# A half-width tile moved from the end of a matmul stage to its start, and the reload behind it

## The reference

```python
x = x + (x @ W.T + b + (x @ (2 * mask - 1)) * coeff)          # layer 0, mask per sequence
def lora_add(base, inp, A, B):                                # A, B picked per sequence
    t = einsum('bri,bni->bnr', A, inp)
    return base + einsum('bor,bnr->bno', B, t) * 0.5
gate = lora_add(x @ W_gate.T, x, A_gate, B_gate)              # 1024 -> 2752
up   = lora_add(x @ W_up.T,   x, A_up,   B_up)
act  = silu(gate) * up
x = x + lora_add(act @ W_down.T, act, A_down, B_down)         # 2752 -> 1024
```

## Time and profile before

| | |
|---|---|
| runs | 1579.68 us median of 3 (1578.99 to 1580.78) |
| span of the profiled execution | 1579.3 us; what lies around the span is not shown apart |
| PE busy | 1545.1 us, 98% |
| DVE, ACT, POOL busy | 1220.1 us (77%), 802.3 us (51%), 426.1 us (27%) |
| moved by DMA | 325.66 MB, 206 GB/s over the span |
| stages | layer 0 to 201 us; block 0 gate/up to 675, down to 889; block 1 gate/up to 1362, down to the end |

### The profile page before, as it was taken

The page is one execution under the profiler, slowest core; times in us unless marked ns, Lnnn a source line. Parts: engine busy times, 40 slices in busy tenths (PEclk is TensorE's granted clock), DMA queues, the critical chain, the costliest instruction groups (busy, mean ns, idle before and its releaser), DMA issues.

```text
span 1579.3 us, 23432 instructions
## 1 busy us (share of the span) xinstructions
PE 1545.1 (98%) x7550; PEld 1304.1 (83%) x7550; DVE 1220.1 (77%) x2136; ACT 802.3 (51%) x1478; POOL 426.1 (27%) x821
## 2 busy tenths in 40 slices
PE   6999998999999999999999989999999999999999
PEld 6999986888888888878888868888888888778887
DVE  8999887676666677688888887767766667798886
ACT  8999855444444444443334464444444444443332
POOL 0000142333333333253410024332323233443100
PEclk9999999999999999999999999999999999999999
DMA  9999854444444444699593725444444445996653
GB/s 372 374 361 376 322 172 127 147 137 154 144 139 155 156 157 153 230 334 312 168 375 111 241 78 168 157 139 134 148 152 148 131 157 179 316 374 220 216 196 116
DMA packets 141961, 325.66 MB, mean 206 GB/s; under 512 B 22416, under 2 KB 50320, under 8 KB 141840
## 3 DMA queue, kind: packets, MB, share of 16 engines
q0 software_dynamic: 61216, 176.21, 33.4%
q1 hardware_dynamic: 76016, 139.57, 26.0%
q10 hardware_dynamic: 4608, 8.39, 1.4%
HBM read 233.51 MB, written 90.18 MB: 205 GB/s over the span
## 4 chain that ended last, share of the span: by engine, by line
PE 87%; DVE 7%; issue 2%; ACT 2%; DMA 1%; SPq 1%; ACTq 0%; POOL 0%; DVEq 0%
PE ps L1509 59%; PE ps L1505 26%; PE ps L1645 2%; DVE m_raw L1135 1%; DVE m_lo L1132 1%; DVE op_b L1132 1%; DMA acc<-x_scratch 1%; DVE acc L1135 1%; DMA m_raw<-in_mask 1%; DVE lo L1132 1%; ACT hi L791 0%; DVE fx L1132 0%; SPq L512 0%; DVE raw L1132 0%; DVE act_t L1306 0%
## 5 line engine op out<-in xcount | busy, mean ns | idle before, releaser
L1509 PE MATMUL ps<-op_b,hi 128*128 128x512 f32 x1616 | 503.4, 393 | 9.3 <-DVE u L1135 5.6
L1132 DVE TENSOR_TENSOR lo<-raw,hi 128x512 fp32r<-128x512 f32 (+2 forms) x640 | 333.4, 530 | 128.7 <-ACT hi L791 126.7
L791 ACT ACTIVATE hi<-raw 128x512 fp32r<-128x512 f32 (+1 forms) x592 | 304.9, 519 | 220.9 <-PE ps L1509 182.9
L1509 PEld LDWEIGHTS ps<-op_b,hi 128*128 128x128 f32 x1616 | 306.0, 190 | 74.1 <-DVE u L1135 6.4
L1509 PE MATMUL ps<-op_b,lo 128*128 128x512 f32 x808 | 318.0, 394 | 0.0
L1509 PE MATMUL ps<-op_d,hi 128*128 128x512 f32 x800 | 248.5, 392 | 4.4 <-DVE acc L1135 4.1
L1505 PE MATMUL ps<-op_b,hi 128*128 128x512 f32 x816 | 252.0, 390 | 0.0
L638 POOL DMA_DIRECT2D operand_scratch<-ot x140 | 75.3, 541 | 552.4 <-DVE ot L1132 536.1
L1135 DVE TENSOR_TENSOR acc<-acc,ps 128x512 f32<-128x512 f32 x248 | 169.9, 685 | 51.0 <-PE ps L1509 43.3
L1509 PEld LDWEIGHTS ps<-op_d,hi 128*128 128x128 f32 x800 | 147.8, 188 | 39.8 <-DVE acc L1135 9.8
L1505 PEld LDWEIGHTS ps<-op_b,hi 128*128 128x128 f32 x816 | 153.4, 188 | 30.7
(11 more groups left out here) (130 smaller groups left out, 2315.9 us busy)
## 6 DMA issues: line engine op xcount, KB each, us to landing
operand_scratch<-ot POOLq DMA_DIRECT2D x140, 512.0 KB, 3.9
op_d<-operand_scratch POOLq DMA_DIRECT2D x140, 512.0 KB, 10.9
raw<-in_wgu SPq DMA_DIRECT2D x168, 256.0 KB, 3.8
m_raw<-in_mask SPq DMA_DIRECT2D x64, 512.0 KB, 5.9
raw<-in_wd SPq DMA_DIRECT2D x160, 128.0 KB, 4.7
w_in<-in_w SPq DMA_DIRECT2D x32, 512.0 KB, 6.7
x_scratch<-x_out POOLq DMA_DIRECT2D x32, 256.0 KB, 4.8
acc<-x_scratch POOLq DMA_DIRECT2D x16, 512.0 KB, 7.5
```

Of the source, the lines that this page charges most:

```text
L791: return nc.scalar.activation(o, i, ACT.Copy)
L1132: return nc.vector.tensor_tensor(o, a, b, ALU.subtract)
L1509: return mm(dst, weight, v, start=False, stop=stop, skip_group_check=True)
```

## The change

The half tile is computed second, right after tile 0, plainly (two "q" steps for each half of the columns, each with the weights of one half of the inner dimension) and in one bank for each half. The adapter's up rows are brought into the form that tiles 2 and later use before tile 1, not between tiles 1 and 2. The operands of down segment 0 have other places in SBUF, so that most of their loads may start earlier in tile 20; the load of acc row 1 is issued after them. Down's banks take turns the other way round. The table b_gu is permuted on the host so that the half tile's adapter rows come second.

```diff
-FUSED = ["q1", "q2", "q3", "q4"]
+HALF_TILE = ["q1", "q2"]
-OPERAND_AT = ["t4", "b11", "t1", "t2", "b22", "t3", "b21"]
+SEG_AT = [{"b11": 8, "t1": 9, "t2": 6, "b22": 7, "t3": 4, "b21": 5, "t4": 10},
+          {"b11": 0, "t1": 1, "t2": 2, "b22": 3, "t3": 11, "b21": 12, "t4": 13}]
 # first_tile_steps: what ACT and DVE do behind a step of PE
-            ("ta", 1, 1): forms("t2", 0, 1, 2, 3) + a_part(1, 6),
-            ("r", 0): [("result", 0)],
-            ("h", 1, 5): [("make4", 2), ("make4", 3)] + forms("t4", 2, 3),
-            ("ta", 1, 7): [("t sum", 1)] + forms("t3", 0),
-            ("g", 1, "p1"): [("t own", 1), ("t high", 1), ("t low", 1)] + forms("t3", 1),
-            ("g", 1, "p5"): [("lora_b", 1)] + forms("t3", 2, 3) + [("make4", 0), ("make4", 1)],
-            ("g", 1, "p6"): forms("t4", 0, 1),
+            ("ta", 1, 1): [("lora_b", PAIRS)] + forms("t2", 0, 1) + a_part(1, 6),
+            ("r", 0): [("result", 0)] + forms("t2", 2, 3),
+            ("h", 1, 5): [("make4", 2), ("make4", 3)],
+            ("ta", 1, 7): [("t sum", 1), ("t own", 1), ("t high", 1), ("t low", 1)],
+            ("q", 0, 0): forms("t3", 0, 1, 2, 3),
+            ("q", 0, 1): [("half result", 0)],
+            ("q", 1, 0): [("make4", 0), ("make4", 1)] + forms("t4", 2, 3),
             ("r", 1): [("result", 1)],
-            ("g", 1, "p3"): [("second result",), ("t neg",)]}
+            ("q", 1, 1): [("half result", 1), ("lora_b", 1)] + forms("t4", 0, 1) + [("half keep", 0), ("half keep", 1)],
+            ("g", 1, "p1"): [("second result",)]}
 # pe_order
-        order += [("g", s, 1, u) for u in PRODUCTS[:3]] + [("r", s, 1)]
-        order += [("g", s, 1, u) for u in PRODUCTS[3:6]] + [("td", s, 0), ("g", s, 1, "p4")]
+        order += [("q", s, 0, 0), ("q", s, 0, 1), ("q", s, 1, 0), ("r", s, 1), ("q", s, 1, 1)]
+        order += [("g", s, 1, u) for u in PRODUCTS[:6]] + [("td", s, 0), ("g", s, 1, "p4")]
-        order += [("g", s, PAIRS, u) for u in FUSED[:2]] + [("td", s, PAIRS - 1)]
-        order += [("g", s, PAIRS, u) for u in FUSED[2:]]
 # POOL, tile 20
-                            pool.wait_ge(pe_done, done["g", s, PAIRS - 1, "p5"])
-                            load_operand(s, 0, "p1")
-                            load_operand(s, 0, "p5")
+                            for u in PRODUCTS[:6]:
+                                pool.wait_ge(pe_done, done["g", s, PAIRS - 1, {"p1": "p5", "p7": "p3", "p2": "p3", "p3": "p6"}.get(u, u)])
+                                load_operand(s, 0, u)
-                pool.wait_ge(ot_l, ot_index[s, KP - 1, "t4"] + 1)
+                pool.wait_ge(pe_done, done["g", s, PAIRS - 1, "p7"])
+                load_operand(s, 0, "p4")
                 load_acc(s, 1)
-                pool.wait_ge(pe_done, done["g", s, PAIRS - 1, "p7"])
-                load_operand(s, 0, "p6")
-                load_operand(s, 0, "p3")
                 ... wait for all stores of ot, load_acc(s, 0) ...
-                load_operand(s, 0, "p7")
-                load_operand(s, 0, "p2")
-                pool.wait_ge(pe_done, done["g", s, PAIRS, "q4"])
-                load_operand(s, 0, "p4")
-                pool.wait_ge(a21_l, HALVES * (s + 1))
+                pool.wait_ge(ot_l, ot_index[s, KP, "b11"] + 1)
                 for h in range(2, HT):
                     load_acc(s, h)
 # ACT
+            def half_result(s, half):
+                act.wait_ge(pe_done, done["q", s, half, 1])
+                if half:
+                    act.wait_ge(a_made, a_count(s, PAIRS, 0))
+                else:
+                    act.wait_ge(form_l, form_count(s, "t3", KQ - 1))
+                nc.scalar.activation(half_silu[HALF:P, :], half_bank(half)[0:HALF, :], ACT.Silu).then_inc(silu_made, 1)
+            def half_keep(s, half):
+                act.wait_ge(a_made, a_count(s, PAIRS, half))
+                act.wait_ge(form_l, form_count(s, "t4", 1))
+                cols = slice(half * N, (half + 1) * N)
+                copy(act_t[0:HALF, cols], half_act(half)[0:HALF, :]).then_inc(half_h, 1)
 # PE
+            def half_part(s, half, part):
+                key, bank = ("g", s, PAIRS, HALF_TILE[part]), half_bank(half)
+                name = (("b11", "b12"), ("b21", "b22"))[part][half]
+                ...
+                for k in range(KQ):
+                    w, i = slice(k * P, (k + 1) * P), op_at(name, k, 0)
+                    mm_new(bank[:, :], high[:, w], op_b[:, i, :], start=k + part == 0)
+                    mm_new(bank[:, :], high[:, w], op_b[:, i + 1, :])
+                    if part and k == KQ - 1:
+                        pe.wait_ge(bw_l, bw_count(s, PAIRS))
+                        pe.wait_ge(t_ready, 4 * s + 2 * half + 2)
+                        for row, t in enumerate((t_gate[half], t_up[half])):
+                            mm_on(bank[:, :], b_w[:, 2 * half + row, :], t[:, :])
+                    end = mm_new(bank[:, :], low[:, w], op_b[:, i, :], stop=part == 1 and k == KQ - 1)
+                end.then_inc(pe_done, 1)
```

More of the change, by code:

```diff
@@ L139, in __init__ @@
                     self.done[self.items[-1]] = self.done["h", key[1], 1, KQ - 1 if u in PLAIN[:2] else HT - 1]
+            elif key[0] == "q" and key[2:] == (0, 0):
+                for part, u in enumerate(HALF_TILE):
+                    self.items.append(("g", key[1], PAIRS, u))
+                    self.done[self.items[-1]] = self.done["q", key[1], 1, part]
             elif key[0] in ("g", "d", "l"):
@@ L184, in place_entries @@
             elif g[0] == "g" and g[2] == PAIRS:
[L185 to L186 removed]
+                names = {WEIGHT[u]: ("a", (*g, u)) for u in HALF_TILE}
             else:
@@ L203, in place_entries @@
         for g in self.groups:
-            if g[0] == "l" or (g[0] == "g" and g[2] == 0):
+            if g[0] == "l" or (g[0] == "g" and g[2] in (0, PAIRS)):
                 continue
-            for name in (["sum", "neg"] if g[0] == "g" and g[2] == PAIRS else ["s1", "s3", "s2", "s4"]):
+            for name in ("s1", "s3", "s2", "s4"):
                 made += 1
@@ L928, in t_gu_high @@
                     copy(dst[R2:2 * R2, :], u2[r:r + R2, :]).then_inc(t_hi, 1)
-            def t_gu_neg(s):
-                act.wait_ge(pe_done, done["r", s, 1])
-                act.wait_ge(t_ready, 4 * s + 4)
-                nc.scalar.activation(t_neg[:, :], t_up[1][:, :], ACT.Copy, scale=-1.0).then_inc(t_neg_ready, 1)
             def first_result(s, half):
@@ L1094, in _ @@
                         form_hi(s, *args)
+                    elif kind == "half result":
+                        half_result(s, *args)
+                    elif kind == "half keep":
+                        half_keep(s, *args)
                     elif kind == "lw":
@@ L1334, in evict @@
                     add(u2[:, :], x_ps[:, :], p5c[:, :]).then_inc(c_made, 1)
+                    if f == 1:
+                        dve.wait_ge(t_moved, 16 * 12 * (s + 1))
+                        sub(t_neg[:, :], t_up[0][:, :], t_up[1][:, :]).then_inc(t_neg_ready, 1)
                     dve.wait_ge(silu_made, silu_count(s, f, 1))
@@ L1553, in first_lora @@
                 end.then_inc(pe_done, 1)
+            def half_part(s, half, part):
+                key, bank = ("g", s, PAIRS, HALF_TILE[part]), half_bank(half)
+                name = (("b11", "b12"), ("b21", "b22"))[part][half]
+                if half and part == 0:
+                    pe.wait_ge(ta_sum, HALVES * s + 1)
+                pe.wait_ge(lo_ready, at[key] + 1)
+                high, low = slot_ap(hi, key), slot_ap(lo, key)
+                for k in range(KQ):
[9 more added lines that the diff above has]
+                end.then_inc(pe_done, 1)
             def gate_up(s, f, u):
@@ L1727, in twice, with in_use_order @@
         return np.concatenate([a, np.split(a, [F - HALF], axis)[1]], axis)
+    def in_use_order(rows):
+        first, pairs, half = np.split(rows, [P, PAIRS * P], 2)
+        return np.concatenate([first, half, pairs], 2)
     x, mask = np.asarray(x), np.asarray(mask_Bx4096x4096_ik1)
```

259 lines of the change are left out of this document (119 added, 140 removed).

## The result

The changed kernel takes 1603.39 us (median of 4 runs, 1601.1 to 1605.94) against 1579.34 us (4 runs) for the kernel before: ratio 1.0151, 95% interval 1.0136 to 1.0165, some 24 us slower. The spans of the two profiled executions are 20.0 us apart, 1599.3 against 1579.3.

A forecast was written before the change was run, and what follows sets the result against it. PE bounds the kernel, busy 1545.1 of 1579.3 us, so savings come from its work or 34 us of standing. Span 1579.3 + 26.4 (down) + 0 (gate stretch) = 1605.7, median 1606 us; range 1586 to 1618.

The forecast's parts named there:

- The sum: Whole kernel: span 1579.3 + 26.4 for down + 0 for the gate stretch = 1605.7, median 1606 us.
- Start of down: Down's first p3 waits 12.6 us for acc row 1; with clock 2.7 and 2.1 regained, 13.2 us a block, 26.4 in all.
- The pace of 1.5 us for each transfer: DMA queue at down's start: 13 transfers of 0.5 MB at 1.5 us each, so acc row 1 lands at 678.3.
- The step that was incomplete: Down's load queue: two stores counted only among 13 transfers ahead of acc row 1; one 12.6 us wait, at p3.
- A term put at nothing: Down's acc row 0: issued right behind row 1, landing one pace later for p6's add, no further wait.
- The queue rival (1593): Down's loads not served in order: p4 waits 6.2 us, 6.8 a block in all, 1593 us; chance 0.15.
- The gate stretch: Around tile 1: block 0 loses 10.2 us against 10.6, block 1 11.1 against 10.3; with matmuls saved, 0 together.
- t_up's wait: Gate stretch, before the adapter's up (r1): the wait of 1.73 us stays as about 1.7, r1 starting at 241.3.
- The other side: Gate stretch gives back all its loss, −21.4 us; with 6.2 us idle at down, 1572 us; chance 0.10.

The follow-up runs named there:

- the run of the order of issue: Changed kernel with GpSimd's earlier issue order for down segment 0 (four operand loads, two stores, acc row 1, then the rest): 1593.74 us, ratio 1.0092.
- the cover put back: Changed kernel with down's very first product computed nine times over in each block, 48 matmuls more where the half tile stood: 1601.63 us, ratio 1.0144.
- the last experiments: Six early loads, new gate order: p1/p5 loads before the t3 store, 1584.13 us; ACT's copy also moved, 1583.03; separately, p7's loads before GpSimd's store wait, 1579.45.
- the order experiments: Gate-stretch operations put behind tile 1's bank copies: on the changed kernel 1600.01 us; with six early loads 1580.69; with tile 0's second result later too 1577.44.
- the last kernels: Changed kernel with six early loads and new gate order, 1580.69 us; that with tile 0's and the half tile's second results one product later, 1577.44 us.
- the fastest kernel: Kernel with six early loads and new gate order, plus tile 0's and the half tile's second results hung one product later: 1577.44 us, ratio 0.9979.
- the kernel of 1580.69: Changed kernel with six early loads, r1 after the last half-tile step, half tile's later copies behind tile 1's bank copies: 1580.69 us, ratio 1.0006.

## Why the prediction was right, step by step

**The sum.** Forecast +26.4, measured +24 in the medians and +20.0 in the spans. By stage, in the spans, down is 23.7 for 26.4 and the gate stretch −3.7 for 0; both are too high, and neither made up for the other. The changed kernel's executions lie 5 us apart (1601.1 to 1605.94), so how the 2.4 us by which the medians fall short divide between the stages is not shown.

**Start of down.** The time from down's start to p3 was forecast as 679.2 − 662.2 = 17.0 us and is 16.4. Of that, 9.64 and 0.93 us are idle, where 12.6 was forecast in one wait, and p6's six matmuls between them ran at half pace; behind p3 the slow clock cost 2.2 us for 2.7. The pace of 1.5 us for each transfer held over the 13 (1.45). Down came out at +12.3 and +11.4 for +13.2 a block. Shown by the order (10 us less with four loads ahead) and by the cover put back (21.8 us of work for nothing).

**The step that was incomplete.** The working followed acc row 1 only and called the two stores in the queue mere length. Their landing frees a slot of ot, ACT's copy of tile 20's last result needs it, and down's p1 copy is behind that one on ACT. So the wait shows at p6 with ACT as releaser, not at p3. Since acc row 1 lands 3 us after p6's late start, the price was the same; with a shorter backlog this could have been a wrong number.

**A term put at nothing.** The prediction has acc row 0 issued right behind row 1, with no further wait. But GpSimd waits for all stores of ot in between, as before. Row 0 was issued 15.4 us after row 1, at 686.47, and landed at 690.6, 2.7 us after it; p6's add followed at 690.62. In block 0 slow matmuls cover this, in block 1 p7 waits 0.76 us. The same wait of GpSimd stands in the way of the last experiments.

**The queue rival (1593)** fell: the stores took 14.3 us behind twelve loads, and acc row 1 landed last and in its turn, 16.8 us after its issue. That the run of the order of issue comes near the same time is another mechanism: the order is kept there and fewer loads are ahead.

**The gate stretch.** Forecast a loss of 10.2 in block 0 against 10.6; measured 8.8 (148 matmuls from 230.99 to 273.57 at 0.228 us). t_up's wait came as forecast (1.73 for 1.7, PE at 241.56 for 241.3). ACT's copy for p6 came at 255.8, p6 at 256.44 for 255.7. PE was ready 2.1 us later than forecast, at 252.5, so the wait was 3.92 and not 5.3. The term missed there is slow matmuls behind the t_up wait; the price after p6 was 1.6 (nine matmuls), not 2.7; the prediction's sentence that a wait of 3 us costs a further 2.7 us was one row made into a rule, and the last section shows waits that cost next to nothing. The forecast of 0 for both blocks was 3.7 too high. That the chain of small operations is the cause is shown by the order experiments. (DVE ot, which the prediction counts once per block, held PE once in all, in block 0.)

**The other side** (waits of the gate stretch gone, 1572) did not come by the change, but the last kernels show that most of that loss can be had back, and that the start of down then eats it: in the fastest kernel the two gate/up stages are 9.4 and 9.0 us shorter than before, and the two down stages 8.1 and 6.5 longer.

**Left open:** how much of the 14.5 us that remain when the order is mended (1593.74 against 1579.22) is the pace of DMA and how much is GpSimd standing in its own waits. In the profiled execution of that run the two down stages are 7.7 and 9.2 us longer than before, and the gate stretches 4.3 shorter together. No run took bytes away.

## What to carry to other kernels

Work at the end of a stage that looks like a remainder can be the cover under which the next stage's loads run. Before moving it, count the transfers that must land by each product and multiply by the pace of the full queue. In an ordered queue, count also what others wait for behind your new loads: stores that free a slot are as urgent as loads. When a trace names one wait, look for the next that ends later behind it before you pay to remove the first.

## What the runs showed of the hardware

An idle time of 1.73 us for t_up is followed in block 0 of the kernel before by matmuls at their usual pace, two in 0.46 us at 243.25. In the changed kernel, after an equal wait at 241.56, about nine matmuls run at half pace, and the clock granted between 241.5 and 253 is 0.85:

```profile
241.50:253.00 11.50, 10.96 (x40) 8.58 (x40) 9.84 (x16) 7.57 (x14) 4.19 (x9) 0.85 0.13 35
```

The 15 matmuls from 241.56 on took 1.7 us too long. Block 1 of the same kernel has the same work and the same wait (1.72 us, at 938.97), and the 15 matmuls behind it take 3.52 us, at full clock:

```profile
938.90:950.00 11.10, 9.39 (x40) 7.44 (x40) 9.48 (x15) 7.38 (x14) 3.31 (x7) 1.00 0.14 33
```

Six kernels here keep t_up's wait after the half tile in both blocks, twelve waits of 1.72 to 1.82 us: behind six of them 15 matmuls take some 5.1 us, behind the other six some 3.5. In the kernel of 1580.69 a wait of 2.89 us in block 0 is followed by a loss of 1.7, and one of 2.86 in block 1 by 0.1. So such a wait may cost its double or not, and neither its length nor its place in the program tells which.

The 512 KB transfers of GpSimd's queue landed in the order of issue, loads and stores alike: of the 296 that load op_d or acc or store ot, none overtook the one before it in either kernel. In the changed kernel's full stretch each took 1.45 us. Behind twelve loads a store takes 14.3 us to land, and behind these and four more transfers a load of acc 16.8; in the kernel before it was 3.0 to 5.0 us for such stores and 5.9 for the same load of acc row 1. The DMA share alone does not tell this: while that load of acc row 1 was on its way it was 1.06 before (659.7 to 665.6) and 1.09 after (671.1 to 687.9).
